# State-space stage: the causal convolution on TensorE, delta times x written over delta, and 12 instead of 14 of 32 state products on GpSimd

## The chip, the cores and the metric

The kernel runs on one core of a Trainium2 chip. The metric is the device time of one execution in microseconds (us). PE is TensorE, DVE is VectorE, ACT is ScalarE, POOL is GpSimd, and SP is the engine whose queue issues all transfers that this text speaks of. All data is fp32.

## What is computed

Four stages follow one another: a state-space stage (changed here), a mixture of experts, a delta-rule stage, and the mixture of experts again. The first stage works on x with 8 batches of 512 positions and 256 features, after a layer norm; there are 512 inner channels, 16 states, 64 ranks of delta and 4 convolution taps. Cut to what matters:

```python
xz = x @ W_in.T
xc, z = jnp.split(xz, 2, axis=-1)
xc = depthwise_causal_conv(xc, conv_w) + conv_b      # 4 taps per channel
xc = silu(xc)
dBC = xc @ W_x.T                                     # delta (64), Bm (16), Cm (16)
delta = softplus(delta @ W_dt.T + b_dt)
deltaA = exp(delta[..., None] * -exp(A_log))
BX = delta[..., None] * Bm[:, :, None, :] * xc[..., None]
hs = scan(h -> deltaA * h + BX)                      # along the positions
y = einsum('bldn,bln->bld', hs, Cm) + Dp * xc
out = (y * silu(z)) @ W_out.T
```

## The kernel before

`mamba_phase` is a hand-ordered program: each engine has its own list, and semaphores tie the lists together. Channels lie on partitions, in `DT` = 4 tiles of 128. The states are worked off in **quads**: quad q covers one channel tile (`dt`) and 4 of the 16 states (`g`), so that a batch has 16 quads and the stage 128. A quad is two **halves**, k = 2q and 2q + 1, and a half is 128 partitions by 2 x 512 elements. In a batch the places are counted as i = k mod 32 on DVE and ACT, and as i = (q + 1) mod 16 on PE.

What one quad takes:

- POOL, `input_quad` (line 368): dx times B for the whole quad into one of 5 ring buffers (`state`). It needs the replicated dx (`dx_rep`), and the sum of quad q - 5 must be done so that the ring buffer is free.
- ACT, `half_decay` (lines 476 to 481): two exponentials per half into a PSUM pair; there are two such pairs, one for even halves and one for odd ones.
- DVE, `half_scan` (line 598): one scan per half. Then the product with C: for halves that `by_pool` picks it is done on POOL (`times_c`, line 377, three quads after the input), for the others on DVE right after the scan (line 605).
- PE, `state_sum` (line 736): sums over the states; its end frees the ring buffer.

`by_pool(k)` picks odd halves except in every eighth quad, which makes 14 of the 32 halves of a batch.

While batch n - 1 is scanned, the next batch n is prepared by pieces that stand between the halves: PE projects x (`project_x`, two tiles after quad 1, two after quad 3), ACT copies each projected tile to `xpad` (three zero columns ahead) and scales it by the last tap (`last_tap`), DVE adds the three other taps (`taps`, line 567: 12 instructions per batch, after i = 10 and i = 14), ACT applies SiLU to all of it at i = 18 (`conv_silu`, `z_silu`, with a table load before and after), PE projects to dt, B and C (`project_dbc`, after quad 6), ACT and DVE make delta by softplus (`softplus_parts`, `softplus_sum`), and POOL multiplies delta by x (`delta_x`, line 357) after quads 14 and 15. SP stores delta and dx to DRAM and loads them back replicated over the states (`store_delta`, `store_dx`, `load_chunk`: 8 transfers of 256 KB for one channel tile). SP issues in order, and an issue that waits holds all that stand behind it. For batch 0 all of this is done ahead of the first quad, tile by tile. After the last batch the stage ends in a barrier.

## Time and profile before

| | us |
|---|---|
| median of 3 runs (2015.22 to 2023.95) | 2016.2 |
| profiled execution, its span | 2017.0 |
| PE busy | 1259.5 |
| DVE busy | 1388.5 |
| ACT busy | 915.8 |
| POOL busy | 1112.5 |

The state-space stage is the first 991 us of the span. The profile names for each group of instructions its line, its engine, the tiles, the count and the mean duration; behind a bar or in square brackets it gives the idle time ahead of the group and the engine or transfer that ended it. "Issue" there stands for a wait whose end the profile puts to nothing. Durations in a row of the timeline run from the first start to the last end of a merged piece, and neighbours on DVE and POOL overlap by some hundredths, so that the pace is read from start to start.

### The profile page before, as it was taken

What the parts mean: (1) busy time and instruction counts of PE and PEld (TensorE: products, weight loads), DVE (VectorE), ACT (ScalarE), POOL (GpSimd) and SP (SyncE); (2) the same over time, 40 slices, a digit from 0 to 9 for tenths busy, and PEclk for the clock granted to TensorE, in tenths of its full rate; (3) what the DMA queues carried; (4) which work ended last, traced back from release to release, by engine and by line L of the source; (5) the groups of instructions that cost most, each with busy time, mean ns of one, the idle gap of its engine ahead of it and who ended that gap; (6) DMA issues with size and microseconds to landing.
All of it is one profiled execution on the core that took longest, in us unless ns stands there. A gap on an engine that the chain in (4) does not pass through costs nothing. (4 is left out here: it accounts for less than half of the span.)

```text
span 2017.0 us, 33672 instructions
## 1 busy us (share of the span) xinstructions
PE 1259.5 (62%) x13844; PEld 595.1 (30%) x13844; DVE 1388.5 (69%) x1689; ACT 915.8 (45%) x1673; POOL 1112.5 (55%) x479
## 2 busy tenths in 40 slices
PE   4464746556474756553488746577767767557875
PEld 1111212121221312120133323244444445443333
DVE  3799999999999999899650023776687668617002
ACT  5555564746556474644232214454455434123220
POOL 1889989899999989999600011322442344412000
PEclk9676768677676777775698877787778777668988
DMA  4827174472808356280299960112312222219997
GB/s 125 198 48 190 45 184 98 102 181 54 206 25 197 84 128 145 54 208 21 93 403 422 421 211 15 43 39 65 76 33 55 65 65 45 65 42 396 405 421 276
DMA packets 193705, 300.04 MB, mean 149 GB/s; under 512 B 82704, under 2 KB 125200, under 8 KB 177168
## 3 DMA queue, kind: packets, MB, share of 16 engines
q1 hardware_dynamic: 188512, 295.17, 48.5%
q10 hardware_dynamic: 4688, 2.19, 0.4%
q8 instruction: 110, 1.80, 0.4%
q0 software_dynamic: 352, 0.52, 0.1%
q14 instruction: 43, 0.35, 0.1%
HBM read 255.37 MB, written 42.47 MB: 148 GB/s over the span
## 5 line engine op out<-in xcount | busy, mean ns | idle before, releaser
L368 POOL TENSOR_TENSOR state<-dx_rep,b_rep 128x2048 f32<-128x2048 f32 x128 | 579.1, 4532 | 66.9 <-PE psum L736 35.7
L736 PE MATMUL psum<-state,sel 128*32 128x512 f32 x1024 | 193.6, 847 | 292.5 <-POOL state L377 292.5
L479 ACT ACTIVATE psum<-delta_rep,a_neg 128x511 f32<-128x511 f32 x512 | 331.5, 684 | 79.8 <-DVE state L598 79.7
L598 DVE TENSOR_TENSOR_SCAN psum<-psum,state 128x1024 f32<-128x1024 f32 x144 | 328.9, 2284 | 33.9 <-POOL state L368 24.0
L598 DVE TENSOR_TENSOR_SCAN state<-psum,state 128x1024 f32<-128x1024 f32 x112 | 255.2, 2279 | 19.9 <-ACT psum L479 19.9
L377 POOL TENSOR_TENSOR state<-state,c_rep 128x1024 f32<-128x1024 f32 x112 | 264.0, 2359 | 0.0
L667 PE MATMUL psum<-xt,w_in 128*128 128x512 f32 x256 | 161.0, 787 | 47.4 <-ACT z_silu L438 26.1
L605 DVE TENSOR_TENSOR state<-psum,c_rep 128x1024 f32<-128x1024 f32 x144 | 176.3, 1224 | 4.9
L736 PEld LDWEIGHTS psum<-state,sel 128*32 128x32 f32 x1024 | 27.5, 128 | 424.4 <-issue 391.4
L476 ACT COPY psum<-zeros 128x2 f32<-128x2 f32 x144 | 23.6, 164 | 257.9 <-DVE state L605 253.2
L1841 PE MATMUL psum<-xt_delta,w_qkv 128*128 128x512 f32 x192 | 111.4, 721 | 12.1 <-DVE attn_t L1655 11.3
L1022 DVE COPY moe_xt<-psum 128x512 f32<-128x512 f32 x16 | 11.1, 691 | 153.2 <-PE psum L1115 153.2
L667 PEld LDWEIGHTS psum<-xt,w_in 128*128 128x128 f32 x256 | 62.9, 259 | 163.8 <-issue 93.0
L1610 DVE SCALAR_TENSOR_TENSOR conv_qkv<-xpad_qkv,conv_w_qkv,conv_qkv 128x512 f32<-128x512 f32 x144 | 97.7, 745 | 15.7 <-ACT conv_qkv L1476 15.4
L1403 POOL TENSOR_TENSOR prod_pool<-t_lane,n_lane 128x1024 f32<-128x1024 f32 x8 | 19.9, 2482 | 151.1 <-DVE t_lane L1627 151.1
L936 ACT ACTIVATE moe_xt<-psum 128x1024 f32<-128x1024 f32 x16 | 16.4, 1024 | 188.8 <-PE psum L1105 188.8
L1625 DVE TENSOR_TENSOR prod<-t_lane,n_lane 128x2 f32<-128x2 f32 (+14 forms) x120 | 49.1, 409 | 68.4 <-DMA n_lane<-n_scratch 65.1
L1367 POOL MEMSET w_gates<- 128x64 f32 x1 | 0.2, 153 | 169.3 <-POOLq L50 169.3
L1125 PE MATMUL psum<-moe_w_set,moe_xt 128*32 128x256 f32 x1024 | 76.2, 439 | 26.5 <-DMA moe_w_set<-in_w 21.1
L1105 PE MATMUL psum<-moe_w_set,moe_merged_g 128*32 128x512 f32 x512 | 77.3, 758 | 24.3 <-DMA moe_w_set<-in_w 24.3
L1475 ACT COPY xpad_qkv<-psum 128x512 f32<-128x512 f32 x48 | 28.2, 587 | 137.6 <-PE psum L1841 137.5
L1420 POOL TENSOR_TENSOR o_delta<-o_delta,o_r 128x1024 f32<-128x1024 f32 x8 | 15.3, 1912 | 117.6 <-ACT o_r L1516 117.6
(218 smaller groups left out, 2535.5 us busy)
## 6 DMA issues: line engine op xcount, KB each, us to landing
moe_w_set<-in_w SPq DMA_DIRECT2D x30, 4096.0 KB, 33.1
delta_rep<-delta_scratch SPq DMA_DIRECT2D x128, 256.0 KB, 5.4
dx_rep<-dx_scratch SPq DMA_DIRECT2D x128, 256.0 KB, 8.2
b_rep<-bc_scratch SPq DMA_DIRECT2D x32, 256.0 KB, 4.9
delta_scratch<-delta SPq DMA_DIRECT2D x32, 256.0 KB, 7.8
dx_scratch<-delta_x SPq DMA_DIRECT2D x32, 256.0 KB, 5.8
c_rep<-bc_scratch SPq DMA_DIRECT2D x32, 256.0 KB, 8.0
moe_x<-x_after SPq DMA_DIRECT2D x16, 512.0 KB, 8.5
```

What stands on the lines that cost most here:

```text
L368: nc.gpsimd.tensor_tensor(ring[q % RING][:, :, :], dx_rep[u % CHUNKS][:, :, :], free_bcast(b_rep[q // QPB % 2][:, g, :], 1, CB), ALU.mult) ...
L377: nc.gpsimd.tensor_tensor(pair, pair, free_bcast(c_rep[b % 2][:, g, :], 1, 2), ALU.mult).then_inc(S["hc_pool"], 1)
L479: ins = nc.scalar.activation(dec[:, i, 1:], delta_rep[u % CHUNKS][:, c, 1:], ACT.Exp, scale=a_neg[:, dt * CB + c, g:g + 1])
L598: nc.vector.tensor_tensor_scan(bx if by_pool(k) else flat, flat, bx, 0.0, ALU.mult, ALU.add).then_inc(S["scan_done"], 1)
L605: nc.vector.tensor_tensor(pair, dec, free_bcast(c_rep[b % 2][:, g, :], 1, 2), ALU.mult).then_inc(S["hc_vector"], 1)
L667: ins = nc.tensor.matmul(bank[:, :], w_in[:, k, tile * P:(tile + 1) * P], xt[:, k, :], start=(k == 0), stop=(k == KD - 1))
L736: ins = nc.tensor.matmul(bank[32 * c:32 * c + 32, :], sel[:, :], ring[q % RING][:, c, :], start=False, stop=(g == NG4 - 1), skip_group_che ...
L1105: ins = nc.tensor.matmul(banks[2 * s + c][j * EQ:(j + 1) * EQ, :], mg[s][:, t, j, :], weights.w1[s][:, j, t, c * BANK:(c + 1) * BANK], sta ...
L1125: ins = nc.tensor.matmul(banks[6][j * EQ:(j + 1) * EQ, 0:D], hid_t[:, k, j * EQ:(j + 1) * EQ], weights.w2[s][:, j, k, :], start=(k == 0), ...
L1610: nc.vector.scalar_tensor_tensor(raw[:, t, :, :], xpad[:, t, :, k:k + P], conv_w[:, t, k:k + 1], raw[:, t, :, :], ALU.mult, ALU.add).then_inc(
L1625: ch.step(nc.vector.tensor_tensor(pr, t_rows, n_row, ALU.mult))
L1841: ins = nc.tensor.matmul(fbank[j % 2][:, :], w_qkv[:, kt, t * P:(t + 1) * P], xt[:, kt, :], start=(kt == 0), stop=(kt == KD - 1))
```

## The change

The convolution moves to PE: each tap is a matmul with a 128 x 128 diagonal matrix (`conv_diag`, built once by DVE from the identity), four per channel tile, summed in PSUM. ACT copies the projected tile to `xpad` and later copies the convolved tile with the bias to `x_conv` (`conv_copy`); the taps leave DVE. The buffer `delta_x` goes: POOL writes delta times x over delta, and so waits until delta has been stored. SP stores delta of two tiles ahead of their dx in batch 0 too. `by_pool` leaves out every fourth quad instead of every eighth: 12 of 32 halves.

```diff
     def by_pool(k):
-        return k % 2 == 1 and (k // 2) % 8 != 7
+        return k % 2 == 1 and (k // 2) % 4 != 3
...
-        dx = m.sb("delta_x", P, DT, L)
+        conv_diag = m.sb("conv_diag", P, DT, KC, P)
...
-                    sp.dma_start(dx_dram[b, t * P:(t + 1) * P, :], dx[:, t, :]).then_inc(S[f"d_stored{t}"], 16)
+                    sp.dma_start(dx_dram[b, t * P:(t + 1) * P, :], delta[:, t, :]).then_inc(S[f"d_stored{t}"], 16)
...
-                for t in range(DT):
-                    store_delta(0, t)
-                    store_dx(0, t)
-                    if t < 2:
-                        load_chunk(0, t)
-                    if t == 0:
-                        load_replicated(0, 1)
+                for pair in ((0, 1), (2, 3)):
+                    for t in pair:
+                        store_delta(0, t)
+                    for t in pair:
+                        store_dx(0, t)
+                        if t < 2:
+                            load_chunk(0, t)
+                        if t == 0:
+                            load_replicated(0, 1)
...
-                    if b:
-                        pool.wait_ge(S[f"d_stored{t}"], 32 * b)
-                    nc.gpsimd.tensor_tensor(dx[:, t, :], delta[:, t, :], xc[b % 2][:, t, :], ALU.mult).then_inc(
+                    pool.wait_ge(S[f"d_stored{t}"], 32 * b + 16)
+                    nc.gpsimd.tensor_tensor(delta[:, t, :], delta[:, t, :], xc[b % 2][:, t, :], ALU.mult).then_inc(
...
+                def conv_copy(b, t):
+                    act.wait_ge(S["conv_psum"], DT * b + t + 1)
+                    nc.scalar.activation(xc[b % 2][:, t, :], xbank(b, t)[:, :], ACT.Identity,
+                                         bias=conv_b[:, t:t + 1]).then_inc(S["conv_done"], 1)
...
                         if i == 10:
-                            last_tap(n, 0)
-                            last_tap(n, 1)
-                        if i == 14:
-                            last_tap(n, 2)
-                            last_tap(n, 3)
+                            xpad_copy(n, 0)
+                            xpad_copy(n, 1)
+                        if i == 13:
+                            conv_copy(n, 0)
+                            conv_copy(n, 1)
+                        if i == 15:
+                            xpad_copy(n, 2)
+                            xpad_copy(n, 3)
+                        if i == 17:
+                            conv_copy(n, 2)
+                            conv_copy(n, 3)
...
-                        if i == 10:
-                            taps(n, (0, 1))
-                        if i == 14:
-                            taps(n, (2, 3))
...
+                def convolve(b, t):
+                    pe.wait_ge(S["xp_read"], DT * b + t + 1)
+                    for j in range(KC):
+                        if b == 0:
+                            pe.wait_ge(S["conv_diag"], KC * t + j + 1)
+                        ins = nc.tensor.matmul(xbank(b, t)[:, :], conv_diag[:, t, j, :], xpad[t % 2][:, j:j + L],
+                                               start=(j == 0), stop=(j == KC - 1))
+                    ins.then_inc(S["conv_psum"], 1)
...
+                        if i == 3:
+                            convolve(n, 0)
+                            convolve(n, 1)
...
+                        if i == 5:
+                            convolve(n, 2)
+                            convolve(n, 3)
```

The order of the transfers of batch 0 on SP, before; the number behind `delta_rep` and `dx_rep` is that of the channel tile:

```order
L275 DMA delta_scratch<-delta 128x512 [waits ma_delta_ready]
L279 DMA dx_scratch<-delta_x 128x512 [waits ma_dx_ready]
L290 DMA delta_rep0<-delta_scratch 32x4x512 [waits ma_d_stored0]
L290 DMA delta_rep0<-delta_scratch 32x4x512 x3
L290 DMA dx_rep0<-dx_scratch 32x4x512 x4
L262 DMA c_rep0<-bc_scratch 32x4x512 x4
L275 DMA delta_scratch<-delta 128x512 [waits ma_delta_ready]
L279 DMA dx_scratch<-delta_x 128x512 [waits ma_dx_ready]
L290 DMA delta_rep1<-delta_scratch 32x4x512 [waits ma_d_stored1]
L290 DMA delta_rep1<-delta_scratch 32x4x512 x3
L290 DMA dx_rep1<-dx_scratch 32x4x512 x4
```

and now, on SP at the same place:

```order
L275 DMA delta_scratch<-delta 128x512 [waits ma_delta_ready] x2
L279 DMA dx_scratch<-delta 128x512 [waits ma_dx_ready]
L290 DMA delta_rep0<-delta_scratch 32x4x512 [waits ma_d_stored0]
L290 DMA delta_rep0<-delta_scratch 32x4x512 x3
L290 DMA dx_rep0<-dx_scratch 32x4x512 x4
L262 DMA c_rep0<-bc_scratch 32x4x512 x4
L279 DMA dx_scratch<-delta 128x512 [waits ma_dx_ready]
L290 DMA delta_rep1<-delta_scratch 32x4x512 [waits ma_d_stored1]
L290 DMA delta_rep1<-delta_scratch 32x4x512 x3
L290 DMA dx_rep1<-dx_scratch 32x4x512 x4
L275 DMA delta_scratch<-delta 128x512 [waits ma_delta_ready] x2
```

The store of delta of tile 1 moved ahead; those of tiles 2 and 3 stay behind the loads of tile 1.

The start of POOL's list, batch 0, before:

```order
L357 TENSOR_TENSOR delta_x<-delta,x_conv 128x512 [waits ma_xc_ready,ma_delta_ready] x4
L368 TENSOR_TENSOR state<-dx_rep,b_rep 128x2048 [waits ma_b_loaded0,ma_dx_loaded0]
L368 TENSOR_TENSOR state<-dx_rep,b_rep 128x2048 x3
L377 TENSOR_TENSOR state<-state,c_rep 128x1024 [waits ma_c_loaded0,ma_scan_done]
L368 TENSOR_TENSOR state<-dx_rep,b_rep 128x2048 [waits ma_dx_loaded1]
```

and now, on POOL at the same place:

```order
L358 TENSOR_TENSOR delta<-delta,x_conv 128x512 [waits ma_d_stored0,ma_xc_ready,ma_delta_ready]
L358 TENSOR_TENSOR delta<-delta,x_conv 128x512 [waits ma_d_stored1,ma_xc_ready,ma_delta_ready]
L358 TENSOR_TENSOR delta<-delta,x_conv 128x512 [waits ma_d_stored2,ma_xc_ready,ma_delta_ready]
L358 TENSOR_TENSOR delta<-delta,x_conv 128x512 [waits ma_d_stored3,ma_xc_ready,ma_delta_ready]
L369 TENSOR_TENSOR state<-dx_rep,b_rep 128x2048 [waits ma_b_loaded0,ma_dx_loaded0]
```

All four products with x, each with the wait for its own store, stand ahead of the first quad.

PE's list in a batch, after the projection of tiles 0 and 1, before:

```order
L736 MATMUL psum<-state,sel 32x512 [waits ma_hc_pool,ma_hc_vector]
L736 MATMUL psum<-state,sel 32x512 x3
L736 MATMUL psum<-state,sel 32x512 [waits ma_hc_pool,ma_hc_vector]
L736 MATMUL psum<-state,sel 32x512 x3
L667 MATMUL psum<-xt,w_in 128x512 [waits ma_conv_done]
L667 MATMUL psum<-xt,w_in 128x512
L667 MATMUL psum<-xt,w_in 128x512 [waits ma_conv_done]
L667 MATMUL psum<-xt,w_in 128x512
```

and now, on PE at the same place:

```order
L739 MATMUL psum<-state,sel 32x512 [waits ma_hc_pool,ma_hc_vector]
L739 MATMUL psum<-state,sel 32x512 x3
L681 MATMUL psum<-xpad,conv_diag 128x512 [waits ma_xp_read]
L681 MATMUL psum<-xpad,conv_diag 128x512 x3
L681 MATMUL psum<-xpad,conv_diag 128x512 [waits ma_xp_read]
L681 MATMUL psum<-xpad,conv_diag 128x512 x3
L739 MATMUL psum<-state,sel 32x512 [waits ma_hc_pool,ma_hc_vector]
L739 MATMUL psum<-state,sel 32x512 x3
L663 MATMUL psum<-xt,w_in 128x512 [waits ma_conv_done]
L663 MATMUL psum<-xt,w_in 128x512
L663 MATMUL psum<-xt,w_in 128x512 [waits ma_conv_done]
L663 MATMUL psum<-xt,w_in 128x512
```

Eight matmuls, held by ACT's copies to `xpad`, now stand between two sums of the states; the same happens with tiles 2 and 3 two quads later.

## Rows read from the trace of the kernel before

**Rows 1.** Windows, one batch: length, busy PE, PEld, DVE, ACT, POOL, clock, DMA, GB/s.

```profile
522.00:638.00 116.00, 69.66 (x224) 24.93 (x224) 110.38 (x82) 69.07 (x124) 108.91 (x35) 0.72 0.51 123
```

**Rows 2.** Timeline of POOL in batch 3: start, length, line, tiles, [idle before].

```profile
405.63 4.50 POOL L368 TENSOR_TENSOR state<-dx_rep,b_rep 128x2048 f32<-128x2048 f32 x1 [3.11 <-issue]
...
430.46 4.52 POOL L368 TENSOR_TENSOR state<-dx_rep,b_rep 128x2048 f32<-128x2048 f32 x1
434.94 2.35 POOL L377 TENSOR_TENSOR state<-state,c_rep 128x1024 f32<-128x1024 f32 x1
437.25 4.52 POOL L368 TENSOR_TENSOR state<-dx_rep,b_rep 128x2048 f32<-128x2048 f32 x1
...
486.59 4.53 POOL L368 TENSOR_TENSOR state<-dx_rep,b_rep 128x2048 f32<-128x2048 f32 x1 [4.05 <-PE psum L736]
...
521.77 4.50 POOL L368 TENSOR_TENSOR state<-dx_rep,b_rep 128x2048 f32<-128x2048 f32 x1 [3.06 <-issue]
```

**Rows 3.** Timeline of DVE in the same batch.

```profile
430.09 2.27 DVE L598 TENSOR_TENSOR_SCAN psum<-psum,state 128x1024 f32<-128x1024 f32 x1
...
435.74 2.27 DVE L598 TENSOR_TENSOR_SCAN psum<-psum,state 128x1024 f32<-128x1024 f32 x1
...
447.77 2.07 DVE L567 SCALAR_TENSOR_TENSOR psum<-xpad,conv_w,psum 128x512 f32<-128x512 f32 x3 [0.96 <-ACT psum L424]
...
462.95 2.72 DVE L567 SCALAR_TENSOR_TENSOR psum<-xpad,conv_w,psum 128x512 f32<-128x512 f32 x4
...
466.90 2.29 DVE L598 TENSOR_TENSOR_SCAN psum<-psum,state 128x1024 f32<-128x1024 f32 x1
...
473.83 2.28 DVE L598 TENSOR_TENSOR_SCAN state<-psum,state 128x1024 f32<-128x1024 f32 x1
...
482.18 2.29 DVE L598 TENSOR_TENSOR_SCAN state<-psum,state 128x1024 f32<-128x1024 f32 x1 [2.62 <-ACT psum L479]
```

**Rows 4.** Timeline of ACT in the same batch.

```profile
444.78 0.59 ACT L423 COPY xpad<-psum 128x512 f32<-128x512 f32 x1 [4.08 <-PE psum L667]
...
475.35 1.28 ACT L434 ACT_TABLE_LOAD   x1
...
480.84 1.30 ACT L479 ACTIVATE psum<-delta_rep,a_neg 128x511 f32<-128x511 f32 x2
```

**Rows 5.** Timeline of PE in the same batch, then windows of PE (length, busy, clock).

```profile
442.79 3.67 PE L667 MATMUL psum<-xt,w_in 128*128 128x512 f32 x8
...
479.19 6.29 PE L696 MATMUL psum<-x_conv,w_x 128*96 128x512 f32 x8 [5.85 <-ACT z_silu L438]
```

```profile
441.70:446.40 4.70, 4.66 (x19) 1.00 0.36 117
...
479.20:485.40 6.20, 6.20 (x8) 0.57 0.00 0
```

**Rows 6.** Stores of delta, single issues: issue ns and place, then time to landing.

```profile
L275 SPq DMA_DIRECT2D delta_scratch<-delta x1: 343/343/343, 498.7 to 498.7; - x1
DMA to landing us min/median/max: 2.7/2.7/2.7
...
L275 SPq DMA_DIRECT2D delta_scratch<-delta x1: 430/430/430, 513.9 to 513.9; - x1
DMA to landing us min/median/max: 8.1/8.1/8.1
```

**Rows 7.** Timeline of the start, all engines.

```profile
13.61 8.74 PE L667 MATMUL psum<-xt,w_in 128*128 128x512 f32 x16 [0.77 <-ACT xt L416]
...
26.70 5.34 PE L696 MATMUL psum<-x_conv,w_x 128*96 128x512 f32 x8 [4.35 <-ACT x_conv L431]
...
37.14 0.34 SPq L275 DMA_DIRECT2D delta_scratch<-delta  x1
37.20 1.27 POOL L357 TENSOR_TENSOR delta_x<-delta,x_conv 128x512 f32<-128x512 f32 x1 [34.99 <-DVE delta L573]
...
42.73 1.74 SPq L290 DMA_DIRECT2D delta_rep<-delta_scratch  x4
...
48.78 0.43 SPq L279 DMA_DIRECT2D dx_scratch<-delta_x  x1
...
54.08 17.88 POOL L368 TENSOR_TENSOR state<-dx_rep,b_rep 128x2048 f32<-128x2048 f32 x4 [8.51 <-DMA dx_rep<-dx_scratch]
...
59.87 1.74 SPq L290 DMA_DIRECT2D delta_rep<-delta_scratch  x4
```

More of the change, by code:

```diff
@@ L416, in xt_copies, with xpad_copy, first_silu @@
                         nc.scalar.copy(xt[:, kt, :], mbank[kt][:, :]).then_inc(S["xt_ready"], 1)
-                def last_tap(b, t):
+                def xpad_copy(b, t):
                     act.wait_ge(S["xp_psum"], DT * b + t + 1)
-                    if b == 0 and t >= 2:
-                        act.wait_ge(S["conv_done"], t - 1)
-                    bank = xbank(b, t)
-                    nc.scalar.copy(xpad[t % 2][:, KC - 1:], bank[:, :])
-                    nc.scalar.activation(bank[:, :], bank[:, :], ACT.Identity, bias=conv_b[:, t:t + 1],
-                                         scale=conv_w[:, t, KC - 1:KC]).then_inc(S["xp_read"], 1)
-                def conv_silu(b):
-                    if b == 0:
-                        for t in range(DT):
-                            act.wait_ge(S["conv_done"], t + 1)
-                            nc.scalar.activation(xc[0][:, t, :], xc[0][:, t, :], ACT.Silu).then_inc(S["xc_ready"], 1)
-                        return
-                    act.wait_ge(S["conv_done"], DT * (b + 1))
+                    if t >= 2:
+                        act.wait_ge(S["conv_psum"], DT * b + t - 1)
+                    nc.scalar.copy(xpad[t % 2][:, KC - 1:], xbank(b, t)[:, :]).then_inc(S["xp_read"], 1)
+                def conv_copy(b, t):
+                    act.wait_ge(S["conv_psum"], DT * b + t + 1)
+                    nc.scalar.activation(xc[b % 2][:, t, :], xbank(b, t)[:, :], ACT.Identity,
+                                         bias=conv_b[:, t:t + 1]).then_inc(S["conv_done"], 1)
+                def first_silu(t):
+                    act.wait_ge(S["conv_psum"], t + 1)
+                    nc.scalar.activation(xc[0][:, t, :], xbank(0, t)[:, :], ACT.Silu, bias=conv_b[:, t:t + 1]).then_inc(
+                        S["xc_ready"], 1)
+                def conv_silu(b):
+                    act.wait_ge(S["conv_done"], DT * b)
                     nc.scalar.activation(xc[b % 2][:, :, :], xc[b % 2][:, :, :], ACT.Silu).then_inc(S["xc_ready"], 1)
@@ L488, in _ @@
                 act.wait_ge(S["conv_loaded"], 16 * 2)
+                for t in range(2):
+                    xpad_copy(0, t)
                 for t in range(DT):
-                    last_tap(0, t)
-                conv_silu(0)
+                    first_silu(t)
+                    if t < 2:
+                        xpad_copy(0, t + 2)
                 nc.scalar.preload_act_table_set("natural_log_exp_and_others")
@@ L556, in norm_shift @@
                                                    ALU.mult).then_inc(S["ln_shift"], 1)
-                def taps(b, pair):
-                    for k in range(KC - 1):
-                        for i, t in enumerate(pair):
-                            if k == 0:
-                                dve.wait_ge(S["xp_read"], DT * b + t + 1)
-                            else:
-                                dve.wait_ge(S["conv_step"], 2 * DT * b + 2 * pair[0] + len(pair) * (k - 1) + i + 1)
-                            bank = xbank(b, t)[:, :]
-                            out = bank if k < KC - 2 else xc[b % 2][:, t, :]
-                            nc.vector.scalar_tensor_tensor(out, xpad[t % 2][:, k:k + L], conv_w[:, t, k:k + 1], bank,
-                                                           ALU.mult, ALU.add).then_inc(
-                                S["conv_step"] if k < KC - 2 else S["conv_done"], 1)
                 def softplus_sum(b, t):
@@ L743, in _ @@
                     project_x(0, t)
+                for t in range(DT):
+                    convolve(0, t)
                 pe.wait_ge(S["proj_loaded"], 16 * 3)
```

17 lines of the change are left out of this document (8 added, 9 removed).

## The prediction

> **What bounds the kernel now.** I read the windows by batch first, then the timelines of POOL and DVE, then those of ACT and PE around the convolution, then SP and the landing of stores, and last the start. The change touches the first 991 us only; the three later stages start behind a barrier and move as one block.
>
> In a batch of 116 us DVE is busy for 110.4 us and POOL for 108.9 [rows 1]: two engines are near their limit. POOL sets the pace. From the first quad of one batch to that of the next it takes 521.77 - 405.63 = 116.1 us [rows 2]. A quad takes it 4.48 us for the input and 2.31 us for a product with C, start to start [rows 2]; 16 and 14 of them and four products with x (1.27 each [rows 7], some 5 us) make 109.0, and two waits the rest: 4.05 us for PE's sum of quad 7, which stands behind a projection that waits for ACT's SiLU [rows 2, 5], and 3.06 us whose end the profile cannot name but which falls where the reloaded dx lands [rows 2]. DVE follows right behind. A quad takes it 5.65 us when POOL has a product of it and 6.93 when it has not, six taps take 3.95 us [rows 3], and it waits some 5.7 us per batch, 0.96 for the taps' input and 2.62 for the decays that ACT makes late because of its SiLU block [rows 3].
>
> **The change part by part, per batch that prepares another (7 of 8).**
>
> *POOL*: two products fewer, 2 x 2.31 = -4.6 us, so 104.4 us of work. The wait for the sum should go, since PE no longer idles ahead of that projection but stays busy from quad 0 on (below).
>
> *DVE*: 12 taps leave, 2 x 3.95 = -7.9 us; two products come, 2 x (6.93 - 5.65) = +2.6. Work falls by 5.3 to 105.1 us.
>
> *DVE's waits*: the taps' own wait of 0.96 goes. But the taps were also a cover. ACT fills the decays of half 11 only after both copies to `xpad`, which wait for PE's projection; in the old kernel DVE did six taps meanwhile. Now it does half 10 alone (3.45 us: a quad of 6.93 has two such halves). Both start when DVE has added the output of an earlier batch: PE then needs 3.67 us [rows 5], the last copy 0.6 [rows 4], two exponentials 1.3 [rows 4], with handovers some 5.8 us. New wait: 5.8 - 3.45 = 2.3 us. Second, ACT's block at i = 18 (from the first table load to the next decays 480.84 - 475.35 = 5.49 us [rows 4]) now comes behind two copies of the convolved tiles at i = 17 and needs PE's z projection, which itself comes behind the convolution of tiles 2 and 3. Following the chain through the rows I get 0.7 us more on the wait of 2.62. Copies on ACT are as many as before (8 for the 4 tiles).
>
> Sum for DVE: -5.3 - 0.96 + 2.3 + 0.7 = -3.3 us, a batch of 112.8.
>
> *PE*: 16 matmuls more, each two records of 3.67 / 8 = 0.46 us at the 2.4 GHz that was granted (1.00) behind a busy stretch [rows 5], so 7.3 us for a pair of tiles and 14.7 per batch. They stand between sums, and a late sum holds POOL's ring: POOL gives a sum about 6.8 us (one quad) before it needs the buffer. With 7.3 us between the sums of quads 2 and 3 I get about 1 us of wait at the input of quad 8, which fits into the room that POOL now has under DVE (112.8 - 104.4).
>
> *The write over delta*: POOL must wait for the store. For tiles 0 and 1 the queue is empty and a store lands in 2.7 us [rows 6], before POOL comes: nothing. For tiles 2 and 3 it is issued behind the 8 reloads of tile 0 and lands in 8.1 us [rows 6]. From delta ready to the next batch's first scan that makes 8.3 + 1.3 + 4.5 = 14.1 us; DVE has from there to the end of its batch halves 27 to 31, 2 x 2.2 + 3 x 3.45 and a gate of 0.6 = 15.4 us. So it costs nothing while DVE sets the pace, with 1.3 us to spare.
>
> *Last batch*: nothing is prepared, POOL sets the pace: -4.6.
>
> *The start* is where the new wait costs. (a) The convolution: before, taps ran while PE was still projecting; now PE projects four tiles until 22.3 [rows 7] and then convolves 32 records of 0.43 to 0.46 us until 36.1 to 37.0. The projection to dt, B, C, which ended at 32.0 [rows 7], ends near 40: +8. (b) Delta of tile 0, stored at 37.14, then at about 45; it lands in 4.5 us (42.73 - 37.14 = 5.6 with dx behind it [rows 7]), then POOL multiplies (1.3), dx lands (2 to 3): the reloads of tile 0 go out at about 53 instead of 42.73. (c) The store of dx of tile 1 lies behind those 8 reloads and 4 of C; the reloads of tile 1 wait for it and go out 59.87 - 42.73 = 17.1 us after those of tile 0 [rows 7]: at 70. (d) Only behind these 8 (3.7 us of issue) do the stores of delta of tiles 2 and 3 stand, and they land 8.1 us later [rows 6]: at 82. POOL's list has the products of tiles 2 and 3 ahead of its first quad, so that starts at 82 + 2.5 = 84.5 instead of 54.08 [rows 7]: **+30 us**, with 26 and 34 as bounds from the rows' spread. Nothing covers it, since every scan waits for it.
>
> Beside (d), the Trainium skill (DMA: Bandwidth & Descriptors, section Anatomy of one DMA — SWDGE (gpsimd) path) gives a transfer a fixed cost of about 2.0 us, mostly the receipt of the last write, plus its bytes at 436 GB/s, which is 2.6 us for 256 KB. By that both stores at the start would land within 3 us of their issue, an estimate that makes the start some 15 us longer and no more; the landing of 8.1 us [rows 6] speaks against it, since there the queue ahead set the time.
>
> **Sum.** 7 x (-3.3) - 4.6 + 30 = +2.3 us on 2017.0, that is 2019.3 for a profiled execution; the median stood 0.8 below it, so 2018.5. The first batch has no output to add and so no wait at half 11, which is 2 us better: **2016.5 us**. The change saves in the loop what it spends at the start.
>
> **The rivals.**
>
> *Faster, the waits don't appear.* If DVE finds its decays ready, POOL becomes the bound: 104.4 + some 6 us of wait for the stores of tiles 2 and 3 = 110.4 us per batch. Then 2016.5 - 7 x 2.4 = 2000. For it: DVE comes 1 us behind POOL now, and a later DVE waits less. Against it: the chain over `xpad` starts at DVE's own output addition, so it moves along with DVE.
>
> *Faster, stores don't queue.* If at the start they land as on an empty queue, 2.7 us [rows 6], (c) shrinks by about 9 and (d) by 5.4: 2002. Against it: the store of dx of tile 1 in the same place took 59.87 - 48.78 = 11.1 us [rows 7].
>
> *Slower, the convolution holds ACT.* The copies at i = 13 and 17 stand in ACT's list ahead of decays. If PE gets the lower clock, a record takes 6.29 / 8 = 0.79 us, as at the granted 0.57 after 5.85 us of idling [rows 5], and a pair of tiles 12.6 instead of 7.3: 5.3 us later. ACT's list has 0.4 us of room at half 14 and DVE waits for the rest: 5 us per batch for one pair, 2016.5 + 35 = 2051, twice that for both. Against it: in the new order PE works nearly without a gap from quad 0 to quad 7, and the clock was full (1.00) [rows 5] in the stretch after such work. It decides from about 0.4 us of lateness. The Trainium skill (TensorE: Matmul & The Clock Gate, Why this matters for your kernels) says that idle gaps between bursts of matmuls bring the clock down; by it the waits for `xpad` are the danger. The rows bear the fall out, but for gaps that the new order mostly closes.
>
> *The wait moves rather than goes.* If the stores of tiles 2 and 3 land some 5 us later than 8.1 in the loop, POOL and not DVE sets the batch, and what POOL was relieved of is given back: 7 x (5 - 1.3) = +26, 2042.
>
> **How the numbers follow.** The forecast has 0.60: its own range of 2002 to 2031 comes from the start's bounds (4 us) and 1.5 us per batch on the two new waits; 0.45 of it lies within 0.5% of 2016.2 (10 us, about what a measurement can tell from no change), 0.06 below, 0.09 above. The waits that don't appear have 0.16, stores that don't queue 0.04, the convolution that holds ACT 0.15, the wait that moves 0.05. Faster is 0.06 + 0.16 + 0.04 = 0.26, the same 0.45, slower 0.09 + 0.15 + 0.05 = 0.29. The range reaches down to the faster rivals and up to the lower slow one: 1999 to 2044.
>
> **What would show it.** Right: POOL's first quad at 80 to 88 us, behind a wait for a store of delta; then batches of 111 to 114 us, a wait of about 2 us of DVE for ACT at half 11 and of 3 at half 19; POOL waiting 5 to 8 us per batch at its last two products with x, and none for the sum of quad 7; matmuls of the convolution at 0.43 to 0.46 us per record. Wrong: a first quad before 75 us (the start is too dear in my sum), batches under 111 (the new waits are not there) or over 115 (ACT is held by the convolution, seen as waits of ACT for PE ahead of its copies).

## The result, and the profile after

The changed kernel took 2024.4 us (median of 20 runs, 2017.0 to 2036.8) and the kernel before 2019.0 us (20 runs, 2011.8 to 2024.5) on the same chip: a ratio of 1.0029, 95% interval 1.0017 to 1.0041. That is within the 0.5% that the prediction called no change. The profiled execution has a span of 2026.2 us against 2017.0. Its state-space stage (to the first instruction of the next stage on POOL) ends at 997.4 us against 994.4; the other 6 us lie in stages whose code is the same, and these differ by as much between the profiles of the other kernels below (1014 to 1027 us from the end of the stage to the last instruction).

So the loop gave back nearly what the start took. The start first: POOL's list, then SP's, columns as in [rows 2] and [rows 7].

```profile
49.13 2.49 POOL L358 TENSOR_TENSOR delta<-delta,x_conv 128x512 f32<-128x512 f32 x2 [46.92 <-DVE delta L572]
80.72 2.48 POOL L358 TENSOR_TENSOR delta<-delta,x_conv 128x512 f32<-128x512 f32 x2 [29.10 <-DMA delta_scratch<-delta]
83.16 8.95 POOL L369 TENSOR_TENSOR state<-dx_rep,b_rep 128x2048 f32<-128x2048 f32 x2
```

```profile
52.40 1.74 SPq L290 DMA_DIRECT2D delta_rep<-delta_scratch  x4
...
57.98 0.43 SPq L279 DMA_DIRECT2D dx_scratch<-delta  x1
68.67 1.73 SPq L290 DMA_DIRECT2D delta_rep<-delta_scratch  x4
70.44 1.86 SPq L290 DMA_DIRECT2D dx_rep<-dx_scratch  x4
72.34 0.96 SPq L275 DMA_DIRECT2D delta_scratch<-delta  x2
```

The first quad starts at 83.16 us instead of 54.08 [rows 7]. The reloads of tile 0 go out at 52.40, the dx of tile 1 waits behind them, its reloads go out at 68.67, and only behind those stand the stores of delta of tiles 2 and 3, which land 8.2 to 8.4 us after their issue and release POOL.

Now the loop. The window of a batch, with the columns of [rows 1]:

```profile
423.00:536.00 113.00, 75.98 (x256) 28.51 (x256) 103.15 (x72) 69.57 (x128) 104.49 (x33) 0.80 0.52 126
```

Against [rows 1] DVE fell from 110.4 to 103.2 us and POOL from 108.9 to 104.5 in a batch, PE rose from 69.7 to 76.0. The batch shrank by less than either: POOL's first inputs of the batches stand at 83.16, 196.01, 310.18, 422.94, 535.95, 650.68, 764.32 and 877.34, which is 113.5 us per batch after the first one, against 116.2 before. What fills the rest is waits: DVE's, then POOL's, in the batch from 423 to 536 (all of POOL's; DVE's but for two of 0.5 to 0.6 us):

```profile
467.82 2.29 DVE L597 TENSOR_TENSOR_SCAN state<-psum,state 128x1024 f32<-128x1024 f32 x1 [2.21 <-ACT psum L482]
...
475.10 0.69 DVE L579 TENSOR_TENSOR z_silu<-psum,z_silu 128x512 f32<-128x512 f32 x1 [1.53 <-PE psum L739]
...
496.62 2.29 DVE L597 TENSOR_TENSOR_SCAN state<-psum,state 128x1024 f32<-128x1024 f32 x1 [2.62 <-ACT psum L482]
...
522.82 2.30 DVE L597 TENSOR_TENSOR_SCAN psum<-psum,state 128x1024 f32<-128x1024 f32 x1 [2.15 <-ACT psum L482]
```

```profile
467.08 4.52 POOL L369 TENSOR_TENSOR state<-dx_rep,b_rep 128x2048 f32<-128x2048 f32 x1 [1.21 <-PE psum L739]
...
475.14 4.53 POOL L369 TENSOR_TENSOR state<-dx_rep,b_rep 128x2048 f32<-128x2048 f32 x1 [1.23 <-PE psum L739]
...
533.49 2.50 POOL L358 TENSOR_TENSOR delta<-delta,x_conv 128x512 f32<-128x512 f32 x2 [6.05 <-DMA delta_scratch<-delta]
```

They are the wait at half 11, which the prediction named; the gate's wait for PE's sum of quad 3, now behind the convolution; the known one at half 19 [rows 3], which didn't grow; and one of 2.15 us at half 26 that nobody had foreseen. POOL waits 1.2 us twice for sums and 6.05 us for the store of delta of tiles 2 and 3. DVE waits for POOL nowhere in the loop.

### The profile page after: what moved, and what is told of

Its sections match the earlier page's. It is cut to its first block and busy times, and to the rows that moved or that the text cites. A ratio compares the mean times of both kernels' runs of the same rounds, so it can differ in the third digit from the quotient of the medians.

```text
span 2026.2 us, 34133 instructions
## 1 busy us (share of the span) xinstructions
PE 1317.7 (65%) x14100; PEld 627.8 (31%) x14100; DVE 1335.6 (66%) x1625; ACT 914.5 (45%) x1685; POOL 1075.5 (53%) x463
## 5 line engine op out<-in xcount | busy, mean ns | idle before, releaser
L597 DVE TENSOR_TENSOR_SCAN psum<-psum,state 128x1024 f32<-128x1024 f32 x160 | 365.1, 2282 | 57.3 <-POOL state L369 33.8
L482 ACT ACTIVATE psum<-delta_rep,a_neg 128x511 f32<-128x511 f32 x512 | 331.4, 684 | 68.8 <-DVE state L597 68.7
L739 PE MATMUL psum<-state,sel 128*32 128x512 f32 x1024 | 182.1, 808 | 210.3 <-POOL state L378 209.9
L597 DVE TENSOR_TENSOR_SCAN state<-psum,state 128x1024 f32<-128x1024 f32 x96 | 218.8, 2279 | 37.4 <-ACT psum L482 37.4
L378 POOL TENSOR_TENSOR state<-state,c_rep 128x1024 f32<-128x1024 f32 x96 | 226.4, 2361 | 0.0
L663 PE MATMUL psum<-xt,w_in 128*128 128x512 f32 x256 | 142.7, 709 | 101.2 <-ACT z_silu L441 47.9
L604 DVE TENSOR_TENSOR state<-psum,c_rep 128x1024 f32<-128x1024 f32 x160 | 195.9, 1224 | 5.5
L681 PE MATMUL psum<-xpad,conv_diag 128*128 128x512 f32 x256 | 115.9, 606 | 3.6 <-ACT xpad L423 3.6
L663 PEld LDWEIGHTS psum<-xt,w_in 128*128 128x128 f32 x256 | 55.4, 227 | 193.8 <-issue 84.8
L358 POOL TENSOR_TENSOR delta<-delta,x_conv 128x512 f32<-128x512 f32 x32 | 40.0, 1270 | 118.5 <-DMA delta_scratch<-delta 71.5
```

The costliest lines, as they stand in the source:

```text
L378: nc.gpsimd.tensor_tensor(pair, pair, free_bcast(c_rep[b % 2][:, g, :], 1, 2), ALU.mult).then_inc(S["hc_pool"], 1)
L482: ins = nc.scalar.activation(dec[:, i, 1:], delta_rep[u % CHUNKS][:, c, 1:], ACT.Exp, scale=a_neg[:, dt * CB + c, g:g + 1])
L597: nc.vector.tensor_tensor_scan(bx if by_pool(k) else flat, flat, bx, 0.0, ALU.mult, ALU.add).then_inc(S["scan_done"], 1)
L604: nc.vector.tensor_tensor(pair, dec, free_bcast(c_rep[b % 2][:, g, :], 1, 2), ALU.mult).then_inc(S["hc_vector"], 1)
L663: ins = nc.tensor.matmul(bank[:, :], w_in[:, k, tile * P:(tile + 1) * P], xt[:, k, :], start=(k == 0), stop=(k == KD - 1))
L681: ins = nc.tensor.matmul(xbank(b, t)[:, :], conv_diag[:, t, j, :], xpad[t % 2][:, j:j + L], start=(j == 0), stop=(j == KC - 1))
```

## The experiments

All ratios are against the kernel before, run beside it on the same chip. "First quad", "batch" (the mean over seven, from POOL's first input of one batch to the next) and "stage end" are from the profiled execution.

| kernel | ratio, 95% interval | median us | first quad | batch | stage end |
|---|---|---|---|---|---|
| before | 1 | 2019 to 2022 | 54.1 | 116.7 | 994.4 |
| changed | 1.0029 (1.0017 to 1.0041) | 2024.4 | 83.2 | 113.5 | 997.4 |
| e1_start_order | 0.9937 (0.9919 to 0.9955) | 2007.8 | 67.5 | 113.6 | 983.2 |
| e2_start_spare | 0.9910 (0.9887 to 0.9933) | 2003.2 | 61.2 | 113.9 | 978.5 |
| e3_xpad11 | 1.0055 (1.0038 to 1.0073) | 2030.4 | 85.3 | 114.7 | 1008.2 |
| e7_soft26 | 1.0004 (0.9982 to 1.0026) | 2018.9 | 84.6 | 113.7 | 1000.7 |
| e4_pool14 | 1.0156 (1.0131 to 1.0181) | 2050.9 | 84.4 | 117.2 | 1028.4 |
| e5_before_pool12 | 1.0133 (1.0115 to 1.0151) | 2045.7 | 55.0 | 119.9 | 1020.9 |
| e6_before_inplace | 1.0210 (1.0191 to 1.0228) | 2060.8 | 76.2 | 119.6 | 1037.6 |
| e8_spare_soft26 | 0.9888 (0.9869 to 0.9906) | 1996.8 | 62.3 | 113.0 | 973.6 |
| e9_act_store | 0.9863 (0.9842 to 0.9884) | 1993.9 | 62.4 | 112.4 | 970.2 |
| e10_pool14_actshift | 1.0125 (1.0091 to 1.0159) | 2045.1 | 87.0 | 115.3 | 1017.5 |
| e11_e8_actshift | 0.9866 (0.9843 to 0.9889) | 1995.2 | 64.0 | 113.0 | 975.2 |
| e12_after_actshift | 1.0019 (1.0001 to 1.0037) | 2023.3 | 85.7 | 112.9 | 995.8 |

### The start, in two ways

e1_start_order puts all four stores of delta of batch 0 ahead of the first store of dx:

```diff
-                for pair in ((0, 1), (2, 3)):
-                    for t in pair:
-                        store_delta(0, t)
-                    for t in pair:
-                        store_dx(0, t)
+                for t in range(DT):
+                    store_delta(0, t)
+                for t in range(DT):
+                    store_dx(0, t)
```

> The changed kernel; only in batch 0 all four stores of delta are issued ahead of the first store of dx. My theory: the 29 us that the start lost are the stores of delta of tiles 2 and 3 standing behind the reloads of tile 1, so POOL's first quad starts at about 63 to 64 us instead of 83.2, the rest is unchanged, and the time falls by 19 to 20 us to about 2005. Rival (the convolution on PE made the start long): the first quad stays above 75 us and the time within 8 us of the changed kernel's 2024.4.

e2_start_spare keeps delta of batch 0: its product with x goes into the last of the 5 ring buffers, which is idle until quad 4, and the old order of stores comes back. Of the edit only that line is shown; `store_dx` reads from the same buffer, POOL waits for the store of delta only from batch 1 on, and quad 4 waits until the four tiles are stored.

```diff
-                    nc.gpsimd.tensor_tensor(delta[:, t, :], delta[:, t, :], xc[b % 2][:, t, :], ALU.mult).then_inc(
+                    nc.gpsimd.tensor_tensor((delta if b else ring[RING - 1])[:, t, :], delta[:, t, :], xc[b % 2][:, t, :], ALU.mult).then_inc(
```

> The changed kernel; in batch 0 alone delta times x is written to the last ring buffer of the states (unused then) and the transfers stand in the order of the kernel before, so nothing of the start waits for a store of delta. My theory: what is left of the start's loss is the convolution, 7 to 8 us; first quad at 61 to 62 us, time 2002 to 2004. Rival (the store wait is not what costs): first quad above 70 us, time above 2012.

Their first quads:

```profile
67.49 17.89 POOL L368 TENSOR_TENSOR state<-dx_rep,b_rep 128x2048 f32<-128x2048 f32 x4 [10.94 <-DMA dx_rep<-dx_scratch]
```

```profile
61.21 17.89 POOL L371 TENSOR_TENSOR state<-dx_rep,b_rep 128x2048 f32<-128x2048 f32 x4 [8.19 <-DMA dx_rep<-dx_scratch]
```

In both, POOL now waits for the reload and no longer for a store. The times fell by 17 and 21 us, about as far as the first quads moved (15.7 and 22.0). Of the 29.1 us at the start, 7.1 (61.21 - 54.08) are therefore the convolution's and 22 the wait for stores. e1 came 4 us later than expected: the four stores and the dx behind them delay the reloads of tile 0 to 55.73.

### The wait at half 11

e3_xpad11 moves ACT's copies of tiles 0 and 1 to `xpad` behind the decays of half 11.

```diff
-                        if i == 10:
+                        if i == 11:
                             xpad_copy(n, 0)
```

> The changed kernel; ACT's copies of tiles 0 and 1 to xpad stand after the decays of half 11 instead of half 10. My theory (DVE sets the pace of a batch, and its wait of 2.2 us at half 11 is lost time): the wait falls below 0.5 us, a batch from 113.0 to 111.0, the time by 11 to 13 us to about 2012. Rival (POOL's wait for the stores of tiles 2 and 3 sets the pace): a batch stays within 0.5 us of 113.0 and the time within 4 us of 2024.4.

The theory failed. The wait at half 11 is gone, but two others grew: at the gate DVE waits 3.62 us instead of 1.53, and in four of the six batches some 1.8 us at half 12.

```profile
479.15 2.30 DVE L597 TENSOR_TENSOR_SCAN psum<-psum,state 128x1024 f32<-128x1024 f32 x1 [1.80 <-ACT psum L482]
```

```profile
DVE z_silu L579 <- PE psum L739: 26.9, 8, 4.0
```

The second row is of the waits from 85 to 1000 us (total, times, longest); the changed kernel has 11.4 us there. The chain from DVE's output addition over PE's projection, ACT's copy, PE's convolution and PE's sum is as long as before: from the end of the addition to the gate it takes 12.94 us in some batches and 14.6 in the others, in both kernels. Moving its middle only changes which instruction of DVE meets it. What made e3 longer lies elsewhere: in its first batch, which has no addition to wait for (116.1 us against 112.8, with 4.01 us at the gate instead of 1.02), and in one batch of 118.5 us, which the last section comes back to.

### The wait at half 26

e7_soft26 moves ACT's softplus of tiles 2 and 3 behind the decays of half 26.

```diff
-                        if i == 25:
+                        if i == 26:
                             softplus_parts(n, (2, 3))
```

> The changed kernel; ACT's softplus of tiles 2 and 3 stands after the decays of half 26 instead of half 25. My theory (DVE sets the pace, and its wait of 2.15 us at half 26 is lost time): that wait goes, delta of tiles 2 and 3 is ready no later than now, a batch falls to 111 us, the time by 13 to 15 us to about 2010. Rival (POOL's wait for the stores sets the pace, and delta of tiles 2 and 3 comes no earlier): batch within 0.5 us of 113.0, time within 4 us of 2024.4.

The wait of 2.15 us at half 26 went in every batch, and the median fell by 0.25%, less than the two intervals can tell apart. What took the rest shows in DVE's waits of the whole loop, 85 to 1000 us:

```profile
DVE psum L597 <- POOL state L369: 41.4, 9, 34.6
```

Beside the one at the start (34.6), DVE now waits for POOL eight times, 0.85 us on average, at half 2 or 4 of six of the seven later batches. In five batches it also waits some 0.96 us for ACT at half 28, and one batch takes 118.8 us, for a reason told in the last section. POOL's own cycle is nearly as long as DVE's.

### One part of the change at a time

e4_pool14 is the changed kernel with 14 products on POOL, e5_before_pool12 the old kernel with 12, both by the one line of `by_pool`. e6_before_inplace is the old kernel with the write over delta, its wait and its order of stores, without the convolution.

```diff
-        return k % 2 == 1 and (k // 2) % 4 != 3
+        return k % 2 == 1 and (k // 2) % 8 != 7
```

> The changed kernel with 14 instead of 12 of 32 products with C on POOL: the convolution and the write over delta without the new share. Theory (DVE and the store chain are about level, and the stretch from the delta of tiles 2 and 3 to the next batch's first scan doesn't depend on POOL's products): two products come back, 2 x 2.31 = +4.6 us of POOL's work, so about 109.1, and DVE's falls from 103.2 to 100.6; POOL's wait for the stores of tiles 2 and 3 (6.0) shrinks by what POOL comes later. Batch 113 to 115 instead of 113.7, last batch +4.6: 0 to +14 us against the changed kernel, so 2024 to 2038. Rival (the products add to the store wait, nothing overlaps): 8 x 4.6 = +37, about 2061. Rival (DVE's products were the price, POOL has room): batch 111, about 2010.

> The old kernel with 12 instead of 14 of 32 products with C on POOL, and nothing else. Theory: DVE's 110.4 us of work grow by 2.6 to 113.0; POOL falls to 104.3 and no longer sets the pace. With the 2 to 5.7 us that DVE waits for ACT the batch is 115 to 118.7 instead of 116.1: 7 x (-1 to +2.6) - 4.6 for the last batch = -12 to +14, forecast +7 us, about 2026. Rival (POOL's relief comes through in full): 8 x -4.6 = -37, 1982.

```diff
-        dx = m.sb("delta_x", P, DT, L)
...
-                    if b:
-                        pool.wait_ge(S[f"d_stored{t}"], 32 * b)
-                    nc.gpsimd.tensor_tensor(dx[:, t, :], delta[:, t, :], xc[b % 2][:, t, :], ALU.mult).then_inc(
+                    pool.wait_ge(S[f"d_stored{t}"], 32 * b + 16)
+                    nc.gpsimd.tensor_tensor(delta[:, t, :], delta[:, t, :], xc[b % 2][:, t, :], ALU.mult).then_inc(
```

> The old kernel (taps on DVE, 14 of 32 products on POOL) with x times delta written over delta, with the wait and the order of stores of the changed kernel, and nothing else. Theory: the start grows by what the convolution leaves of the 29 us, 29 - 7 = 22 (first quad at 76 instead of 54.08); in the loop POOL paces, and a wait of 3 to 6 us for the stores of tiles 2 and 3 comes on it, 7 x 3 to 7 x 6 = +21 to +42: 2063 to 2083. Rival (in the loop the store wait takes the place of the 3.06 us that POOL waited there before): +22 alone, 2041.

The write over delta alone costs 2.1%, just below the range expected (2060.8 us against 2063 to 2083): 22.1 us at the start, then batches of 119.6 us. The convolution on top of it (e4 against e6) gives back 0.5%, the two products on top of both another 1.3%. Yet the same two products cost 1.3% when they come to DVE without the taps leaving it (e5, 2045.7 us against a forecast of 2026): DVE had 110.4 us of work there and got 2.6 more. A batch of e5 shows that its waits grew too, at the taps from 0.96 [rows 3] to 3.09 us:

```profile
459.67 0.76 DVE L567 SCALAR_TENSOR_TENSOR psum<-xpad,conv_w,psum 128x512 f32<-128x512 f32 x1 [1.74 <-ACT psum L424]
461.78 2.07 DVE L567 SCALAR_TENSOR_TENSOR psum<-xpad,conv_w,psum 128x512 f32<-128x512 f32 x3 [1.35 <-ACT psum L424]
```

e4 lay between my theory and the rival. Its trace had something that explained it, so it seemed: DVE's smallest instruction took 12.43 us.

```profile
411.04 2.28 DVE L597 TENSOR_TENSOR_SCAN state<-psum,state 128x1024 f32<-128x1024 f32 x1
413.24 12.43 DVE L567 SCALAR_TENSOR_TENSOR neg_mean_rstd<-mean_var,rstd 128x4 f32<-128x4 f32 x1
425.58 2.29 DVE L597 TENSOR_TENSOR_SCAN psum<-psum,state 128x1024 f32<-128x1024 f32 x1
```

```profile
418.85 4.50 POOL L369 TENSOR_TENSOR state<-dx_rep,b_rep 128x2048 f32<-128x2048 f32 x1
423.30 2.34 POOL L378 TENSOR_TENSOR state<-state,c_rep 128x1024 f32<-128x1024 f32 x1
431.89 2.49 POOL L358 TENSOR_TENSOR delta<-delta,x_conv 128x512 f32<-128x512 f32 x2 [6.25 <-DMA delta_scratch<-delta]
```

It ends at 425.67 (413.24 + 12.43), just where POOL runs out of work (423.30 + 2.34 = 425.64).

### Is it that instruction, or POOL's work?

e10_pool14_actshift, e12_after_actshift and e11_e8_actshift compute that shift on ACT, in e4's kernel, in the changed kernel, and in e8's (below).

```diff
-                    nc.vector.scalar_tensor_tensor(nmr[:, :], mv[:, :, 0], -1.0, rstd[:, :], ALU.mult,
-                                                   ALU.mult).then_inc(S["ln_shift"], 1)
...
+                    nc.scalar.activation(nrstd[:, :], rstd[:, :], ACT.Identity, scale=-1.0).then_inc(S["ln_neg"], 1)
+                    act.wait_ge(S["ln_neg"], b + 1)
+                    for st in range(ST):
+                        ins = nc.scalar.activation(nmr[:, st:st + 1], mv[:, st, 0:1], ACT.Identity,
+                                                   scale=nrstd[:, st:st + 1])
```

> The changed kernel with 14 of 32 products on POOL, as in the run that took 2050.9 us, but with the layer norm's shift (minus mean times rstd, 128x4) computed by ACT in five small instructions instead of by DVE in one. In that run DVE's one instruction took 43.0 us in 7 times (0.14 to 12.45 us each, until POOL was idle), against 4.0 us in the changed kernel. Theory (DVE's instruction, whose two inputs both lie in SBUF, is held while POOL works, and that made most of the 26 us that the two products cost): without it the batch falls from 117.2 to 113 to 114.5 us, 2020 to 2032. Rival (POOL's own work of 109 us and its waits set the batch, the hold was only idle time put into another place): 2045 to 2052.

> The changed kernel with nothing but the move of the layer norm's shift to ACT: the control for the run with 14 products. DVE's instruction took 0.14 us in 6 of 7 times there, so nothing is gained but some 3 us in batch 0; five instructions of 0.2 us on ACT ahead of half 26, where DVE already waits 2.15 us for ACT, cost 7 x 1.0. Theory: 2024 to 2031. With the run of 14 products it gives the price of the two products alone: by the hold theory 0 to 8 us, by the rival 20 to 27.

The theory of the hold fell. With no such instruction on DVE, 14 products still cost 1.06% more than 12 (1.0125 against 1.0019, some 21 us), as the rival said; the move to ACT by itself cost nothing that can be measured (e12 against the changed kernel), and the hold was 2 us per batch in the profiled executions (117.2 to 115.3), while the medians, 2050.9 and 2045.1 us, have intervals that overlap. What sets the pace is POOL's own cycle. POOL and SP in a batch of e10:

```profile
528.46 2.56 POOL L359 TENSOR_TENSOR delta<-delta,x_conv 128x512 f32<-128x512 f32 x2
530.91 4.58 POOL L370 TENSOR_TENSOR state<-dx_rep,b_rep 128x2048 f32<-128x2048 f32 x1
535.38 2.42 POOL L379 TENSOR_TENSOR state<-state,c_rep 128x1024 f32<-128x1024 f32 x1
544.03 2.48 POOL L359 TENSOR_TENSOR delta<-delta,x_conv 128x512 f32<-128x512 f32 x2 [6.23 <-DMA delta_scratch<-delta]
```

```profile
529.81 1.55 SPq L280 DMA_DIRECT2D dx_scratch<-delta  x2
531.83 1.77 SPq L291 DMA_DIRECT2D delta_rep<-delta_scratch  x4
533.64 1.85 SPq L291 DMA_DIRECT2D dx_rep<-dx_scratch  x4
535.54 0.91 SPq L276 DMA_DIRECT2D delta_scratch<-delta  x2
```

The wait of 6.2 us isn't a wait for DVE. It begins with POOL itself: its product for tiles 0 and 1 (528.46) lets SP store dx and issue the 8 reloads, and the stores of delta of tiles 2 and 3, which stand behind these, land and let POOL go on at 544.03. That takes 15.6 us here, 15.4 in the changed kernel (518.13 to 533.49), 15.2 to 16.0 in the batches of e4 and e6, whatever DVE does; POOL has 9.3 us of work in it. In e10's batches from 200 us on POOL waits for no sum, so its cycle is its work and that wait: 109.0 + 6.2 = 115.2, the batch shown (the mean of seven is 115.3). With 12 products these two make 104.5 + 6.05 = 110.6, and 2.44 us of waits for sums fill the batch of 113.0; those hang on the other engines too. How far they give way, e7 shows:

```profile
473.23 4.53 POOL L369 TENSOR_TENSOR state<-dx_rep,b_rep 128x2048 f32<-128x2048 f32 x1 [0.26 <-PE psum L739]
...
481.29 4.52 POOL L369 TENSOR_TENSOR state<-dx_rep,b_rep 128x2048 f32<-128x2048 f32 x1 [1.23 <-PE psum L739]
```

Once DVE came earlier, the first of the two fell from 1.21 to 0.26 us and the second stayed; the three batches with such a row took 112.0 to 112.6 us. So with 12 products POOL has about 1 us of room below the 113.0, and no more.

### Versions that beat both

e8_spare_soft26 joins the edits of e2 and e7; e9_act_store adds to it that ACT and not SP issues the stores of delta of tiles 2 and 3 in the loop:

> The changed kernel with both edits that gained when each was alone: batch 0's product with x in the idle sixth buffer of the ring, and the softplus of tiles 2 and 3 one half later. Theory (the two are in different stretches, start and loop, and add): 2003 - 5 = about 1998, first quad at 61, batches of 112.3. Rival (POOL's store chain takes back all that the later softplus gives): 2003, batches of 113.5.

```diff
+                        if i == 27:
+                            for t in (2, 3):
+                                act.wait_ge(S["delta_ready"], DT * n + t + 1)
+                                act.dma_start(delta_dram[n, t * P:(t + 1) * P, :], delta[:, t, :]).then_inc(S[f"d_stored{t}"], 16)
```

> The kernel of the run before (spare buffer at the start, softplus of tiles 2 and 3 one half later), with the stores of delta of tiles 2 and 3 in the loop issued by ACT at half 27 instead of by SP behind the 8 reloads of tile 0. It asks whether a store waits because it stands behind the reloads in one queue, or because the transfers are busy whatever the queue. Theory (the queue): from another queue the store lands about 3 us after its issue instead of 8, POOL's wait of 6 us falls to 1 to 2, DVE no longer waits for POOL (0.9 per batch), and the batch falls from 112.3 to 111.3: 7 x -1 = -7, about 1990. Rival (the 16 engines are shared, the store lands 6 to 8 us after its issue as before): the wait stays at 5 to 6 and the time at 1997; and if issuing costs ACT time, half 28's decays come later, up to +1 per batch, 2004.

> The kernel with the spare buffer at the start and softplus of tiles 2 and 3 after half 26 (1996.8 us), with the same move of the layer norm's shift to ACT. There DVE's instruction was held once, for 4.60 us, the other times it took 0.14. Theory: the held batch loses 4 us and ACT has 1 to 3 us of idle time at half 25, so the five instructions cost nothing: 1993. Rival (they come on DVE's waits for ACT, 7 x 1): 2000 to 2004.

e8 gave what the sum of both said, 1996.8 us, 1.1% faster than the kernel before. On the question of e9 the rival holds where a store goes out together with the reloads: from a queue of its own it lands no sooner. Its two issues:

```profile
L531 ACTq DMA_DIRECT2D delta_scratch<-delta x2: 326/326/326, 502.9 to 503.5; - x2
...
DMA to landing us min/median/max: 7.9/8.0/8.0
```

SP had issued the last of the 8 reloads at 503.2 there. In the changed kernel the first of the two stores went out 1.9 us after the last reload and landed in 6.3, in e7 right behind it and landed in 8.4: in each case about 8 us after the last reload was issued. So behind the reloads it is their traffic that a store waits out, and not the queue. The test is narrow, though: in six of seven batches ACT's first store went out within 0.1 us of SP's last reload. In the seventh it went out 1.2 us ahead of it (issue done at 840.0 against 841.2) and landed sooner:

```profile
L531 ACTq DMA_DIRECT2D delta_scratch<-delta x2: 327/338/348, 839.6 to 840.2; - x2
...
DMA to landing us min/median/max: 6.5/7.0/7.5
```

```profile
846.26 1.27 POOL L358 TENSOR_TENSOR delta<-delta,x_conv 128x512 f32<-128x512 f32 x1 [2.96 <-DMA delta_scratch<-delta]
```

POOL waited 2.96 us there instead of 5.5 to 6.5. Whether a second queue and an earlier issue would save half of that wait in every batch is not shown. e9 and e11 are not told apart from e8 (their intervals overlap).

## Why the prediction was right, and where its steps were off

**The time.** 2016.5 forecast for a kernel before of 2016.2, no change; measured no change, 0.3% slower and inside the range. The three large terms held: +30 us at the start (29.1), -25 over the seven batches that prepare another (-22.7, from 816.85 to 794.18 us between the first inputs of the first and the last batch), -4.6 in the last one (POOL's first input to its last instruction, 108.6 to 104.0; 3.4 of it reach the end of the stage).

**The start.** Each station was within 1.5 us: the projection to dt, B and C ended at 39.3 (40 forecast), reloads of tile 0 at 52.4 (53), of tile 1 at 68.7 (70), the stores landed at 80.7 (82). The rival in which stores don't queue is out. The estimate that the prediction took from the Trainium skill (DMA: Bandwidth & Descriptors, section Anatomy of one DMA — SWDGE (gpsimd) path), stores landing within 3 us, did not hold for these: 8.2 to 8.4 us. That section gives its figure for transfers that GpSimd issues; these are issued by SP, behind 8 others.

**The loop: a right sum of partly wrong terms.** DVE's batch was forecast at 112.8 and came to 113.5. Its work fell by 7.2 us instead of 5.3; the wait at half 11 was sized right (2.21 against 2.3) for three of its six batches; half 19 didn't grow (0.7 forecast). The 2 us that the median forecast took off for the first batch were 0.7 (112.9 against 113.5). Missed were 1.53 us at the gate, since PE's sum of quad 3 stands behind eight convolution matmuls, and 2.15 us at half 26. The larger fall of DVE's work and the wait at half 26 belong together: DVE's tiny instruction for the layer norm took 2.21 us in the old kernel, from 504.81 to the end of a product that POOL ran until 507.0, and 0.14 in the new one, where it falls on the border of two instructions of POOL. POOL and DVE, before and then now:

```profile
504.66 2.33 POOL L377 TENSOR_TENSOR state<-state,c_rep 128x1024 f32<-128x1024 f32 x1
504.81 2.21 DVE L555 SCALAR_TENSOR_TENSOR neg_mean_rstd<-mean_var,rstd 128x4 f32<-128x4 f32 x1
```

```profile
518.13 2.52 POOL L358 TENSOR_TENSOR delta<-delta,x_conv 128x512 f32<-128x512 f32 x2
520.54 0.14 DVE L567 SCALAR_TENSOR_TENSOR neg_mean_rstd<-mean_var,rstd 128x4 f32<-128x4 f32 x1
```

Its 2.1 us had covered ACT's softplus, so what left DVE's work came back as a wait. One more term stood nowhere in the sum: in the old kernel DVE waited 0.85 to 1.05 us for POOL at half 4 of each batch but the first, and that wait went:

```profile
423.82 2.30 DVE L598 TENSOR_TENSOR_SCAN psum<-psum,state 128x1024 f32<-128x1024 f32 x1 [1.05 <-POOL state L368]
```

So the sum missed -1.9 (work), -0.7 (half 19) and -1.05 (half 4) on one side, and +1.53 (gate) and +2.15 (half 26) on the other. Apart from the 2 us that changed their name, that these cancel to within 0.7 us is luck. I had asked what the taps covered, and not what else changes when engines shift against each other.

**POOL.** The work was right (104.5 against 104.4), the store wait too (6.05 for 5 to 8), the wait for the sum of quad 7 went. The waits for sums behind the convolution were 2.44 us instead of 1, and 3.15 to 3.85 in the three batches in which the clock fell (below). The step that failed is "it costs nothing while DVE sets the pace, with 1.3 us to spare": I counted the store wait from DVE's delta, but it is tied to POOL's own product for tiles 0 and 1, so it is a fixed 6 us of POOL's cycle. With the waits for sums POOL's batch is full at 113.0, and e7 shows that only about 1 us of it gives way: it took DVE's wait away and ran into POOL.

**The rivals.** The waits appeared, so the first is out; its POOL cycle (110.4) lacked the waits for sums, 1.5 us even in e7's best batches, so that it could have given no 2000 us. The matmuls of the convolution ran at 0.45 us per record (7.13 for 16) at a granted clock of 1.00. ACT did wait for them ahead of its copies at i = 13 and 17, the sign of being wrong that the prediction named, 85 to 1000 us:

```profile
ACT x_conv L427 <- PE psum L681: 18.4, 14, 2.0
```

But no scan of DVE behind these copies waits for its decays: at i = 13 DVE stands at the gate for the same convolution (475.10 above), and halves 14 and 18 follow without a gap. So the wait came, and it cost nothing. The clock did show at another place, at half 11. The projection of tiles 0 and 1 after 2.4 to 2.9 us of idling takes 3.67 us in three of six batches and 5.32 to 5.37 in the others:

```profile
349.50:353.17 3.67, 3.67 (x12) 1.48 (x16) 3.29 (x2) 0.58 (x1) 3.61 (x1) 1.00 0.42 143
575.00:580.40 5.40, 5.38 (x12) 2.08 (x16) 3.31 (x2) 0.58 (x1) 3.87 (x1) 0.68 0.29 97
```

The clock is the last column but two: 1.00 is 2.4 GHz throughout, 0.68 a stretch of which part ran at 1.2 GHz. DVE's wait at half 11 is 2.21 us in the first three and 3.86 to 3.90 in the others, which is most of the spread between batches of 112.8 and 114.7. Why the clock fell in one batch and not in the next, after idle times as long, stays open.

## What to carry to other kernels

A buffer that is saved by writing over an input turns a store into a wait, and the wait lasts as long as the transfers issued just ahead of that store (here about 8 us behind 8 of 256 KB): look at the start, where nothing covers it, and ask whether some other buffer is idle at that time (here it was, and gave 1%). Share work between two engines only when you know both cycles with their fixed waits: the same two products were worth -1.1% with the taps gone from DVE and +1.3% with them still there. When a wait is moved, follow the chain to its end; if its length is unchanged, another instruction will meet it.

## What the runs showed of the hardware

An instruction of DVE on 128x4 elements whose two inputs both lie in SBUF took 0.14 us when it met the border of two instructions of POOL, 2.2 us in the old kernel, 4.60 in e8, 6.90 in e7 and up to 12.45 in e4. In the state-space stage of every kernel that has it, all but the first (POOL is idle then) ended within 0.07 us of the end of an instruction of POOL: in e8 it ran to the end of one input,

```profile
497.62 4.60 DVE L569 SCALAR_TENSOR_TENSOR neg_mean_rstd<-mean_var,rstd 128x4 f32<-128x4 f32 x1
```

```profile
497.71 4.49 POOL L371 TENSOR_TENSOR state<-dx_rep,b_rep 128x2048 f32<-128x2048 f32 x1
```

and in e4 through several that followed one another, until POOL had nothing to do. Why it got through at the next border in e8, and not in e3, e4 and e7, stays open. DVE's other instructions in the loop, which have at most one tensor input in SBUF, show nothing of the kind: the scans' mean is 2.28 us in both kernels. The Trainium skill (SBUF — State Buffer, section SBUF: two separate sides) says that GpSimd and a DVE instruction with two SBUF inputs contend for a shared port pair, which the one that starts first keeps for its whole instruction. The traces agree with the hold, but 12.43 us across several instructions of POOL is more than one whole instruction, and there the measurement decides. The long batches of e3 (118.5 us), e7 (118.8) and e8 (117.1) each follow on such a hold, of 6.92, 6.90 and 4.60 us.

Whether a batch is held there seems to hang on some 10 ns. In the changed kernel DVE's gate and POOL's input start on the same sum of PE (475.10 and 475.14 above, and within 0.05 us in all seven batches), so that 45 us later DVE's instruction comes each time just ahead of the same border of POOL. It came 0.11 to 0.12 us before the end of POOL's instruction and passed; the three that were held in e3, e7 and e8 came 0.12 to 0.13 us before it. (In e5, where the two run differently, one was held that came 0.07 us before it, so this is not the whole rule.) That the changed kernel was not held there in its profile is luck.

Second, a store of 256 KB behind 8 reloads landed about 8 us after the last reload's issue, from the same queue (8.4) and from another engine's (8.0) alike; the one that another engine issued 1.2 us ahead of the last reload landed 4.9 us after it.
